# One block instead of two: convolution, node rows and attention without a barrier between them, a moved jump, and a new order of the node rows

## The reference

```
h   = x @ W_in + b_in                                   # layer 0, a continuous-filter convolution
Wij = (ssp(f_ij @ Wf1 + bf1) @ Wf2 + bf2) * rcut[:, None]   # ssp(v) = softplus(v) - ln 2
agg = segment_sum(h[idx_j] * Wij, idx_i)                # idx_i = src, idx_j = dst
x   = layernorm(x + ssp(agg @ Wo1 + bo1) @ Wo2 + bo2)

h_att = x @ Watt + batt                                 # layer 1, attention over the same edges
e     = leaky_relu(h_att[src] @ a1 + h_att[dst] @ a2, 0.2); e = e - max(e)
alpha = exp(e) / (segment_sum(exp(e), dst)[dst] + 1e-9)
neigh = segment_sum((x @ W1 + b1)[src] * alpha, dst)
x     = layernorm(x + leaky_relu(x + neigh + (x * neigh) @ W2 + b2, 0.2))
```

## Time and profile before

| | us |
|---|---|
| median of three runs | 1439.12 |
| the profiled execution | 1441.44 |
| its span, first to last instruction | 1439.7 |
| PE, DVE, ACT, POOL busy | 1186.2, 1204.4, 859.6, 840.4 |
| last back load issued by SP | 1103.70 |
| start of POOL's last scatter | 1109.88 |
| last sum on DVE ends | 1111.64 |
| SP's skip over further rounds, branch to next branch | 1112.3 to 1112.8 |
| first late load issued by SP | 1120.01 |
| first late load issued by ACT | 1123.9 |
| chunk 0 of the late loads used by DVE | 1126.66 |
| barrier passed, first product of the second block | 1123.08 |
| lowest score known on DVE | 1198.17 |
| first `weights` on DVE | 1216.59 |
| end | 1439.7 |

### The profile page before, as it was taken

How to read it: one execution, slowest core, us unless ns; L and a number is a source line. 1 busy time by engine, 2 the same in 40 slices (tenths; PEclk the granted TensorE clock), 3 DMA queues, 4 the chain that set the end, 5 groups by cost and what they waited for, 6 DMA issues and landing times. The chain is left out here.

```text
span 1439.7 us, 28075 instructions
## 1 busy us (share of the span) xinstructions
PE 1186.2 (82%) x9129; PEld 960.1 (67%) x9129; DVE 1204.4 (84%) x2206; ACT 859.6 (60%) x2140; POOL 840.4 (58%) x922
## 2 busy tenths in 40 slices
PE   4778877788999769999799999999877594788895
PEld 3444545456888648777587777777666483787895
DVE  8798866558999769999799999999956468999984
ACT  1556564576888878879888888888653143000032
POOL 4167777777777777777777777777656221000021
PEclk9689887899999999999999999999989796889997
DMA  7233342368898578996799978988775880866650
GB/s 258 67 80 96 84 121 70 84 164 215 223 259 244 160 221 233 275 241 200 206 274 251 247 207 245 267 232 243 217 206 148 223 264 0 257 228 224 236 188 27
DMA packets 246739, 276.50 MB, mean 192 GB/s; under 512 B 35121, under 2 KB 194511, under 8 KB 243252
## 3 DMA queue, kind: packets, MB, share of 16 engines
q1 hardware_dynamic: 200128, 185.24, 43.7%
q10 hardware_dynamic: 20596, 35.89, 12.2%
q0 software_dynamic: 25856, 53.42, 11.5%
HBM read 163.26 MB, written 111.20 MB: 191 GB/s over the span
## 5 line engine op out<-in xcount | busy, mean ns | idle before, releaser
L1884 POOL DMA_INDIRECT edge_rows<-x_rows,pos x808 | 783.1, 969 | 298.3 <-issue 228.8
L1404 ACT ACTIVATE h_edge<-ps_wh,w_col 128x128 f32<-128x128 f32 x808 | 229.4, 367 | 128.9 <-PE ps_wh L1196 122.6
L1240 PEld LDWEIGHTS ps_d<-back_one,back 128*128 128x128 f32 x1914 | 236.4, 196 | 73.9 <-issue 70.1
L1240 PE MATMUL ps_d<-back_one,back 128*128 128x128 f32 x1914 | 246.3, 282 | 17.4 <-DVE agg_t L1702 16.9
L1203 PE MATMUL ps_wh<-wf,filt 128*128 128x128 f32 x1616 | 238.7, 293 | 1.3 <-DVE filt L1504 1.3
L1189 PE MATMUL ps_v<-f_t,wf 128*128 128x512 f32 x400 | 221.6, 637 | 0.0
L1508 DVE TENSOR_TENSOR x_rows<-ps_wh,h_edge 128x512 f32<-128x512 f32 x202 | 138.0, 683 | 96.2 <-ACT h_edge L1404 41.0
L1203 PEld LDWEIGHTS ps_wh<-wf,filt 128*128 128x128 f32 x1616 | 209.6, 203 | 3.3 <-DVE filt L1504 3.3
L1037 PE MATMUL ps_wh<-yard 128*128 128x150 bf16 x1575 | 138.4, 233 | 64.3 <-DVE yard L1027 34.1
L1037 PEld LDWEIGHTS ps_wh<-yard 128*128 128x128 bf16 x1575 | 109.1, 100 | 109.0 <-DVE yard L1027 78.9
L2347 PE MATMUL ps_wh<-loan,yard 128*126 128x129 f32 x1250 | 152.9, 285 | 33.8 <-DVE yard L2590 25.9
(11 more groups left out here) (335 smaller groups left out, 1490.1 us busy)
## 6 DMA issues: line engine op xcount, KB each, us to landing
c_tab<-yard SPq DMA_DIRECT2D x25, 1575.0 KB
yard<-c_tab SPq DMA_DIRECT2D x25, 1575.0 KB, 6.6
dst_bc<-dst ACTq DMA_DIRECT2D x99, 252.0 KB
back<-edge_rows SPq DMA_DIRECT2D x42, 516.0 KB
edge_rows<-x_rows,pos POOLq DMA_INDIRECT x808
back<-edge_rows SPq DMA_DIRECT2D x48, 258.0 KB
m_tab<-yard SPq DMA_DIRECT2D x25, 393.8 KB
mask_room<-m_tab SPq DMA_DIRECT2D x5, 1968.8 KB, 12.7
```

Of the source, the lines that this page charges most:

```text
L1240: mm = nc.tensor.matmul(acc(c), back[:, n % BR, k0 + t, 0:D], back_one[:, m % 2, o + t, :], start=t == 0, stop=t == k1 - k0 - 1, skip_grou ...
L1404: copy = nc.scalar.activation(h_edge[:, j, q, :], ps_wh[:, bank, 1, q * D:(q + 1) * D], ACT.Copy, scale=w_col[:, t(q)])
L1884: return pool.indirect_dma_start(table[s], bass.IndirectOffsetOnAxis(places_here, 0), rows, None)
```

## The change

Four things are changed.

1. The second block is gone: its code stands in the same block as the convolution's. In place of the barrier, DVE writes one element (`conv_end`) behind its convolution and raises a semaphore `ended`; ACT and POOL wait for it before their first instruction of the node rows, SP only before it loads x.
2. Convolution is cut at half `MID` = 101. `If(n_win < 2)` holds the first 101 halves, then come the general path and its jump, then a second `If(n_win < 2)` holds the rest. The number of passes and rounds is loaded into registers in mid-convolution, and the skips over further rounds and passes stay at the end.
3. DVE takes the messages out of PSUM itself and adds the biases in the same instruction (two for a chunk, 128 x 390 and 128 x 260). ACT's ten copies and POOL's six additions are gone.
4. The hand-written orders of PE, ACT and DVE in the node rows are new, ACT's softplus does its Relu third instead of first, and the masked passes have `EARLY = 2`, `TWICE = 8`: two ahead of unit 0, two behind each of eight units. `TOP_AT` stays 15.

```diff
-EARLY = 1
-TWICE = 6
+EARLY = 2
+TWICE = 8
...
-            block = conv.enter_context(nc.Block())
+            block = steps.enter_context(nc.Block())
...  (SP; PE, ACT and DVE alike)
                 with sp.If(n_win < 2):
-                    one_window()
-                    sp.wait_ge(back_out, len(SETS))
-                    sp.wait_ge(rk, RK_ALL)
-                    n_round = value(sp, rounds[0:1, 0:1], RMAX + 1, 1)
-                    with sp.If(n_round > 1):
-                        all_added(sp, NH)
-                        more_rounds(n_round - 1, 0)
+                    one_window(range(MID // 2))
                 with sp.If(n_win > 1):
                     more_windows()
...
+                sp.wait_ge(pick_done, 1)
+                n_pass = value(sp, passes[0:1, 0:1], MAXP + 1, 1)
+                with sp.If(n_win < 2):
+                    sp.wait_ge(rk, RK_ALL)
+                    n_round = value(sp, rounds[0:1, 0:1], RMAX + 1, 1)
+                    one_window(range(MID // 2, NG))
+                    rest_of_window()
+                    with sp.If(n_round > 1):
+                        sp.wait_ge(back_out, len(SETS))
+                        all_added(sp, NH)
+                        more_rounds(n_round - 1, 0)
...
+                nc.vector.memset(conv_end[:], 0.0).then_inc(ended, 1)
...
-            block = nodes.enter_context(nc.Block())
...  (SP, POOL, ACT)
+                sp.wait_ge(ended, 1)
                 sp.dma_start(x1[0:Q, :, :], a["x_rows"][0:QN, :]...).then_inc(x_in, 16)
...  (DVE)
+                def message_rows(c):
+                    dve.wait_ge(msg_mm, c + 1)
+                    for k, n in ((0, 3), (1, 2)):
+                        at = c * CB + 3 * k
+                        ins = nc.vector.tensor_tensor(msg_sb[:, at:at + n, :], msg_bank(k).rearrange("p (b d) -> p b d", b=n),
+                                                      b1_b[:, :].unsqueeze(1).to_broadcast([P, n, MR]), ALU.add)
+                    ins.then_inc(msg_done, 1)
...  (PE)
-                sums(4)
                 z(1)
+                sums(4)
                 o1(3)
+                z(2)
                 turn(0)
-                z(2)
                 o1(4)
                 z(3)
-                s2(0)
                 turn(1)
                 z(4)
+                s2(0)
                 message(0)
...
```

More of the change, by code:

```diff
@@ L839, in _ @@
                 assert ranked[0] == RK_PREP
+        steps = ctx.enter_context(ExitStack())
+        ended = sem("ended")
         with ExitStack() as conv:
@@ L1294, in count_all, with one_window @@
                     pe.wait_ge(c_sb, NGR)
-                def one_window():
-                    rows_part(0)
-                    for k in range(HALVES + 1):
+                def one_window(halves):
+                    for k in halves:
                         if k < NH:
-                            if k:
-                                rows_part(k)
+                            rows_part(k)
                             filter_part(k)
@@ L1356, in _ @@
                 with pe.If(n_win < 2):
-                    one_window()
-                    pe.wait_ge(rk, RK_ALL)
-                    n_round = value(pe, rounds[0:1, 0:1], RMAX + 1, 1)
-                    with pe.If(n_round > 1):
-                        more_rounds(n_round - 1, 0)
+                    one_window(range(MID))
                 with pe.If(n_win > 1):
@@ L1367, in _ @@
                     more_rounds(n_round, (NS - 1) * NB)
+                pe.wait_ge(pick_done, 1)
+                n_pass = value(pe, passes[0:1, 0:1], MAXP + 1, 1)
+                with pe.If(n_win < 2):
+                    pe.wait_ge(rk, RK_ALL)
+                    n_round = value(pe, rounds[0:1, 0:1], RMAX + 1, 1)
+                    one_window(range(MID, HALVES + 1))
+                    with pe.If(n_round > 1):
+                        more_rounds(n_round - 1, 0)
                 pe.wait_ge(c_sb, NGR)
                 pe.wait_ge(h_copied, NH)
-                n_pass = value(pe, passes[0:1, 0:1], MAXP + 1, 1)
                 with pe.If(n_pass > 1):
@@ L1438, in put_lo, with one_window @@
                                                 ACT.Copy)
-                def one_window():
-                    softplus(1, 0)
-                    for k in range(HALVES + 1):
+                def one_window(halves):
+                    for k in halves:
+                        if k == 0:
+                            softplus(1, 0)
                         if k % 2 == 0 and k + 4 < NH:
@@ L1735, in first_places, with one_window @@
                     place(0).then_inc(pos_put, 1)
[L1737 to L1743 removed]
+                def one_window(halves):
+                    for k in halves:
+                        if k == 0:
+                            onehots(0)
+                            first_places()
+                            filters(0)
+                            for g in groups_at(0):
+                                count_group(g, iota_lo_ps, iota_key_ps)
                         if k + 1 < NH:
@@ L1849, in _ @@
                     more_rounds(n_round, (NS - 1) * NB)
+                n_pass = value(dve, passes[0:1, 0:1], MAXP + 1, 1)
+                with dve.If(n_win < 2):
+                    n_round = value(dve, rounds[0:1, 0:1], RMAX + 1, 1)
+                    one_window(range(MID, HALVES + 2))
+                    dve.wait_ge(back_out, len(SETS))
+                    with dve.If(n_round > 1):
+                        for s in range(NS):
+                            w0, w1 = LOOPS[s]
+                            ins = past(s, slice(s * NB + w0, s * NB + w1), 1)
+                        ins.then_inc(m_past, 1)
+                        dve.wait_ge(m_past, 1)
+                        more_rounds(n_round - 1, 0)
                 dve.wait_ge(c_mm, NGR)
                 dve.wait_ge(c_sb, NGR)
-                n_pass = value(dve, passes[0:1, 0:1], MAXP + 1, 1)
                 with dve.If(n_pass > 1):
@@ L2102, in build @@
             KEPT = NC - 2
-            BESTS = [EARLY + 3 + min(2 * n, n + TWICE) for n in range(NB)]
-            TOP_AT = NB - EARLY - 3 - TWICE
+            BESTS = [EARLY + min(2 * n, n + TWICE) for n in range(NB)]
+            TOP_AT = NB - EARLY - TWICE
             FROM = TOP_AT + 3
@@ L2184, in _ @@
             def _(pool):
+                pool.wait_ge(ended, 1)
                 all_added(pool, NH)
@@ L2195, in _ @@
                     refined(pool, mv, c, stats_done, rough, refine, rstd_done, 0)
-                for c in range(NC):
-                    pool.wait_ge(msg_copied, c + 1)
-                    for cols in ((slice(MR - 1, MR), slice(0, MR - 1)) if c == NC - 1 else (slice(0, MR),)):
-                        rows = msg_sb[:, c * CB:(c + 1) * CB, cols]
-                        nc.gpsimd.tensor_tensor(rows, rows, b1_b[:, cols].unsqueeze(1).to_broadcast(
-                            [P, CB, cols.stop - cols.start]), ALU.add).then_inc(msg_done, 1)
                 for c in range(NC):
@@ L2703, in _ @@
                 finish_rows(NC - 1)
+        steps.close()
 def kernel(**inputs):
```

107 lines of the change are left out of this document (46 added, 61 removed).

## The result

The changed kernel takes 1424.91 us (median of six runs, 1422.64 to 1432.27), the kernel before 1438.53 us beside it (six runs, 1435.20 to 1440.89). The ratio is 0.9905, 95% interval 0.9884 to 0.9926, so by the medians it is faster by 13.6 us (by the interval 10.6 to 16.7 us, about 1%); 1424.7 us were predicted, -14.4 us.

What follows compares the result with a forecast made beforehand. POOL's indirect DMAs pace the convolution, then a PE, ACT, POOL and DVE chain, then DVE. Terms -6.8 + 0 - 7.3 + 0.9 - 1.2 = -14.4 us took 1439.1 to 1424.7 us, range 1420 to 1433.

Steps and rivals of the forecast that it cites:

- End of the convolution: From POOL's last scatter to SP's first late load: load waits for the last landing alone, 6.8 us saved, ends 5.8 and 7.6.
- Jump in mid-convolution: Near 580 us, PE, ACT, DVE and SP jump; covered by DVE's work ahead, costing 0, ends 0 and +5 us.
- Node rows: End of sums(3) to lowest score: new order keeps PE at full clock, 7.3 us saved, ends 3.4 and 7.6.
- Messages on DVE: DVE takes messages from PSUM; the fifth chunk stands alone behind the lowest score, +0.9 us, ends 0.7 and 1.2 per chunk.
- first pass: First masked pass on DVE without POOL's last bias additions: 3.44 us instead of 4.69, so -1.2 us.
- Masked passes: Two passes move from ahead of the first weights to behind units 6 and 7 on the same full engine: 0.
- The lower end of the range, 1420: Whole kernel's best time, from both parts at their good ends, 7.6 and 7.6 + 1.2.
- The signs on the clock of the span: In the new trace: lowest score some 14 us earlier, first weights some 21, unit 15 some 14.
- the node rows give little: Rival, node rows: a late turn makes PE wait over 4 us and lose clock; 1428.6 us, chance 0.17.
- the skips stall: Rival, end of convolution: each remaining skip costs DVE 3.2 us, gain there shrinks to about 4.9; 1426.6 us, chance 0.08.
- `ended` or a landing would hold SP as long as the barrier did: Rival, end of convolution: SP held as before, so only the node rows count; 1431.5 us, chance 0.07.
- Slower: Rival, mid-convolution: slow instruction fetches at the jump starve POOL; with a 35 us stall 1447 us, chance 0.04.

Runs made afterwards that it cites:

- nodes_only: The kernel before with the new node rows alone (two blocks, jump at the end, no `ended`): 1434.5 us, ratio 0.9936 to before.
- jump_end: The changed kernel with all halves in the first branch, so the jump stands behind the last half, in one block: 1434.28 us, ratio 0.9931 to before.
- again: The changed kernel run once more, unchanged: median 1428.95 us against 1444.79 for the kernel before, ratio 0.9896.
- two_blocks: The changed kernel with a second block again, so with the barrier between convolution and node rows: 1431.88 us, ratio 0.9911 to before.
- messages_back: The changed kernel with ACT copying the messages and POOL adding the biases again, PE's new order kept: 1790.15 us on a slower chip, ratio 0.9886 to before.
- four_ahead: The changed kernel with four masked passes ahead of unit 0 and six times two behind (`EARLY = 4`, `TWICE = 6`): ratio 0.9914 to before, slower chip.
- x_last_s4: The changed kernel with x loaded behind the late loads of chunks 3 and 4, and PE's fifth sums ahead of z(1): 1787.9 us, slower chip, ratio 0.9858.
- mid_60: The changed kernel with the jump over the general path at half 60 instead of 101: ratio 0.9924 to before, on a slower chip.
- x_last: The changed kernel with the load of x behind the late loads of chunks 3 and 4: 1790.57 us on a slower chip, ratio 0.9886 to before.
- x_mid: The changed kernel with the load of x between the late loads of chunks 3 and 4: 1790.92 us on a slower chip, ratio 0.9883 to before.

## Why the prediction was right, point by point

**End of the convolution, -6.8: the gain came, its size was that of one trace, and its way was only half told.** Shown: the first late load comes 2.6 to 4.5 us behind the last scatter in all eleven traces in which SP does not wait for the last sums, predicted 3.3. Before, it came 8.4 to 8.6 us behind the end of the last sum, and that sum ended 1.8 us behind S in the trace that I had, 1.3 us ahead of S in nodes_only and 6.6 us behind it on a slower chip. So the term depends on the execution: 7.2 - 4.5 = 2.7 us at the least on the first kind of chip, 6.7 between the first two traces. By the medians this part is 5.6 us, with intervals that overlap. My ends, 5.8 and 7.6, were too narrow, because I took 1111.64 as if it were fixed to the last scatter. I had also said that what follows starts as many us earlier as the first load does. It doesn't: in jump_end the first load is 3.9 us behind S and the fourth sums end at 41.1, in nodes_only 7.2 and 40.9. The later loads count as well, and ACT's wait for `ended`. That the jump's place matters through DVE's `ended` (jump_end) I had not said; I had counted SP's and PE's jumps only, and called ACT's wait harmless, which it is only once DVE's jump is gone.

**Jump in mid-convolution, 0: right near the jump; over the whole convolution a debt of 2 us is not excluded.** Timelines of PE, ACT and DVE of the changed kernel, and POOL's waits from 575 to 640 us:

```profile
584.01 0.64 PE L1210 MATMUL ps_wh<-h_win,onehot_t 126*128 126x128 bf16 x4 [5.21 <-issue]
...
585.30 1.14 ACT L1419 ACTIVATE h_edge<-ps_wh,w_col 128x128 f32<-128x128 f32 x4 [6.06 <-PE ps_wh L1210]
...
583.89 0.41 DVE L1518 TENSOR_SCALAR onehot_t<-dst_bc,base_p,win_off 126x512 bf16<-126x512 int16 x1 [2.39 <-issue]
```

```profile
POOL edge_rows L1907 <- issue: 14.0, 45, 0.6
POOL edge_rows L1907 <- DVE x_rows L1527: 1.8, 6, 0.3
```

Gaps of 5.2, 6.1 and 2.4 us (3.4, 4.6 and 1.3 in again) lie side by side, and POOL never waits over 0.3 us for DVE. DVE's is below the 3 to 6 us predicted: its sequencer goes from the branch at 577.97 to the next instruction at 582.46, 4.5 us, but four instructions on `yard` issued before it still run until 581.5. ACT's is a wait for PE. PE's granted clock from 582 to 600 us was 0.84, where it was 1.00 before; POOL, which sets the pace there, started 15 scatters in both. What the jump cost came out of DVE's waits for landings, as I had said: 6.2 us from 582 to 820 where they were 13.7.

```profile
DVE x_rows L1527 <- DMA edge_rows<-x_rows,pos: 6.2, 4, 2.1
```

The other traces agree: 9.7 and 8.3 us with the jump in the middle (again, two_blocks), 13.4 and 12.8 us with it at the end (nodes_only, jump_end).

**Node rows, -7.3: right.** The lowest score is known at t = 1188.78 - 1152.53 = 36.3 (35.8 predicted, 43.1 before), so 6.9 us. sums(4) at 5.5, turn(0) at 13.2, s2(0) at 21.0, turn(3) at 25.4 and turn(4) at 28.8 lie within 0.2 us of the order followed. messages_back splits it: 2.4 us of the whole are the messages' new place. The rest is left for the order by subtraction; the old order with the messages on DVE was not run.

**Messages on DVE, +0.9, and first pass, -1.2: right** to 0.03 us (0.90 and 3.44 in the rows above). From the lowest score to the first weights it is 11.4 us, predicted 11.3.

**Masked passes, 0: right**, shown by four_ahead within 0.8 us. All of it behind the fourth sums is 61.5 - 47.6 = 13.9 us, less 6.6 for the two passes: 7.3 us, predicted 7.3 - 0.9 + 1.2 = 7.6.

**The sum.** The median moved by 13.6 us where 14.4 were predicted, and by 15.8 in again. That the first is within 1 us is in part luck: one term was read from one trace and can be anything from 3 to 7 us, and the time ahead of S, which the sum puts at nothing, differs by several us from execution to execution. The lower end of the range, 1420, does not follow from the good ends either: with 7.6, 7.6, 1.2 and 0.7 for the messages they give 1423.4. The signs on the clock of the span came smaller than predicted for the same reason: the first weights 16.4 us earlier in the first trace and 19.7 in again's, not 21. The two traces differ by only 9.8 us because their last scatters lie 4.7 us apart. Of these, 2.1 us are there already at the 360th scatter (533.26 and 531.17), ahead of the jump; for the other 2.6 nothing shows an effect of the change. The three traces with the jump in the middle have S at 1114.59, 1110.19 and 1114.83, the three with it at the end 1109.88, 1110.86 and 1108.11, but if each is moved by the distance from its traced execution to its kernel's median, it is 1110.2 and 1112.9 for again and two_blocks, 1114.1 and 1113.7 for jump_end and nodes_only, and 1107.2 and 1107.0 for the changed kernel and the one before. That is an estimate, since it puts all the spread ahead of S.

**The rivals.** That the node rows give little is excluded (PE waits 0.3 us in 36.3). That the skips stall is half true: DVE's two skips take 2.1 to 2.9 us of issue on the first chips (0.9 to 1.9 on the slower ones) where I priced about 1, and PE's 5.1 us where it took 4.20, but both are over before chunk 0 is there, so no cost can be seen. The Trainium skill ("Runtime: NRT & Kernel Launch", Instruction fetch mechanics) says that a taken branch out of the pages held forces a fetch; these gaps, and the 10.2 us in jump_end, agree with it, though no run shows the fetch alone. That `ended` or a landing would hold SP as long as the barrier did is excluded by SP's row. Slower is excluded by POOL's waits near the jump.

## What to carry to other kernels

A jump over unused code is paid by the engine that makes it and by all that wait for that engine, so put it where the engine that sets the pace has work in stock, and list the waiters of every engine that jumps. A term read from a distance between two engines at a stage's end has to be split into what is fixed (8.4 us behind the last sum) and what moves from run to run (where that sum lies), or its range is too narrow. While the DMA engines are full, order the loads by when their data is first used, and then move the compute that would wait (x_last_s4, shown in its trace and not secured by its median).

## What was not expected of the hardware

Two of the three chips of the experiments run the convolution a third slower: in mid_60 the last scatter starts at 1480.50 us instead of 1110. Between 800 and 1033 us, which holds other halves in the two, again first and mid_60 second (waits of POOL, of PE's weight loads and of PE):

```profile
POOL edge_rows L1907 <- DVE x_rows L1527: 4.1, 12, 0.8
...
PEld ps_wh L1042 <- DVE yard L1032: 23.9, 39, 1.2
```

```profile
POOL edge_rows L1907 <- DVE x_rows L1527: 67.8, 20, 8.3
...
PEld ps_wh L1042 <- issue: 43.8, 26, 12.1
...
PE ps_wh L1042 <- issue: 17.1, 14, 2.9
```

The single instructions take as long as on the first chips (one of POOL's 0.96 us, one to x_rows 0.69), the DMA share is 0.56 (0.86 in again), and PE's granted clock there is 0.87 (0.99). PE stands still without a wait that the profile shows, also between matmuls of one product. Instruction fetches do not take longer as packets (mean 1.13 us in mid_60, 1.12 in again). What holds the sequencers stays open. Behind the convolution the same chips give 47.6 us for the node rows like the others.

When an addition on POOL runs beside DVE, both are slowed. POOL's five additions of the bias to x take 7.5 us in x_last and 10.14 us in x_mid, where DVE's one-hot of chunk 4 ran beside them and took 4.09 us for 2.83 us alone.
